# A depthwise convolution on TensorE: from full-array matmuls to sixteen 32x32 tiles

## What is computed

```python
def _L2_conv_ref(x, w77, b77, w53, b53, w35, b35, w7w, w7h, w5w, w5h):
    bias = (b77 + b53 + b35)[None, :, None, None]
    out = dwconv(x, w77, 3, 3) + dwconv(x, w53, 2, 1) + dwconv(x, w35, 1, 2) \
        + dwconv(dwconv(x, w7w, 0, 3), w7h, 3, 0) + dwconv(dwconv(x, w5w, 0, 2), w5h, 2, 0) + bias
    return out
```

## Time and profile before

| | us |
|---|---|
| median of 3 runs | 4579.74 |
| lowest, highest | 4578.52, 4580.29 |
| the profiled execution | 4581.92 |
| its span in the profile | 4580.3 |
| PE busy, share of the span | 4151.4, 91% |
| the depthwise layer in the span | about 2829 to 3219 |

### The profile page before, as it was taken

One profiled execution on the slowest core, in us unless ns is written; L12 is line 12 of the kernel. 1 busy time (PEld: TensorE's weight loads), 2 busy tenths in 40 slices (PEclk: granted clock), 3 DMA queues, 4 the chain that ended last, 5 costly groups with the idle time before them and its releaser, 6 DMA issues. The chain is left out here.

```text
span 4580.3 us, 47617 instructions
## 1 busy us (share of the span) xinstructions
PE 4151.4 (91%) x13451; PEld 2549.2 (56%) x13451; DVE 3146.5 (69%) x3239; ACT 2284.8 (50%) x3612; POOL 1357.1 (30%) x994
## 2 busy tenths in 40 slices
PE   6999999999999999569999995797499999999999
PEld 5777777777776767324344442786244444444444
DVE  4758575767676767567777663244488788888878
ACT  2858585858585858333332211211255445445544
POOL 2858585848584858121111101110000000000000
PEclk8999999999999999779999997898699999999999
DMA  4333332333332323211111011232301100110110
GB/s 129 84 100 91 94 94 92 93 95 93 93 96 85 99 83 103 77 55 42 42 42 42 28 55 58 77 113 89 145 0 41 41 15 26 41 41 0 41 41 14
DMA packets 116343, 308.02 MB, mean 67 GB/s; under 512 B 47088, under 2 KB 48752, under 8 KB 106560
## 3 DMA queue, kind: packets, MB, share of 16 engines
q1 hardware_dynamic: 110880, 294.50, 20.4%
q0 software_dynamic: 3840, 11.01, 1.1%
q10 hardware_dynamic: 1440, 0.16, 0.0%
HBM read 198.24 MB, written 106.85 MB: 67 GB/s over the span
## 5 line engine op out<-in xcount | busy, mean ns | idle before, releaser
L451 POOL TENSOR_TENSOR probs_lo<-probs,probs_hi 128x512 fp32r<-128x512 f32 x848 | 1178.5, 1404 | 651.0 <-ACT probs L497 628.6
L557 DVE TENSOR_REDUCE maxima<-m_psum 128x1 fp32r<-128x1024 f32 x528 | 644.4, 1221 | 371.9 <-PE m_psum L725 371.1
L496 ACT ACTIVATE probs_hi<-s_psum 128x512 fp32r<-128x512 f32 x1024 | 613.1, 599 | 389.0 <-PE o_psum L754 226.6
L2306 PE MATMUL psum<-mixes,conv_t 128*128 128x512 f32 x1728 | 751.1, 592 | 0.0
L497 ACT ACTIVATE probs<-s_psum 128x512 f32<-128x512 f32 x1024 | 608.7, 594 | 0.0
L2306 PEld LDWEIGHTS psum<-mixes,conv_t 128*128 128x128 f32 x1728 | 327.5, 190 | 409.8 <-issue 409.8
L738 PE MATMUL s_psum<-q_all,k_hi 128*128 128x512 f32 x1026 | 426.6, 416 | 21.5 <-ACT probs L497 21.3
L754 PE MATMUL o_psum<-probs_lo,v 128*112 128x512 f32 x1024 | 412.0, 402 | 14.6 <-DVE probs_lo L637 7.7
L739 PE MATMUL s_psum<-q_all,k_lo 128*128 128x512 f32 x1026 | 404.2, 394 | 0.0
L749 PE MATMUL o_psum<-probs_hi,v 128*112 128x512 f32 x1024 | 403.2, 394 | 0.0
L725 PE MATMUL m_psum<-k_hi,q_all 128*128 128x512 f32 x1056 | 353.6, 417 | 32.4 <-DVE maxima L557 19.2
(11 more groups left out here) (324 smaller groups left out, 6556.4 us busy)
## 6 DMA issues: line engine op xcount, KB each, us to landing
xin<-in_x SPq DMA_DIRECT2D x17, 1536.0 KB, 7.2
xin<-x SPq DMA_DIRECT2D x17, 1536.0 KB, 6.8
k_hi<-k_rows_hi SPq DMA_DIRECT2D x134, 192.0 KB, 3.4
xres<-x SPq DMA_DIRECT2D x16, 1536.0 KB, 7.1
xb<-x SPq DMA_DIRECT2D x4, 4096.0 KB, 15.9
k_rows_hi<-stage_hi SPq DMA_DIRECT2D x54, 256.0 KB, 2.1
k_rows_lo<-stage_lo SPq DMA_DIRECT2D x54, 256.0 KB, 2.3
q_rows_hi<-stage_hi SPq DMA_DIRECT2D x52, 256.0 KB, 2.5
```

Of the source, the lines that this page charges most:

```text
L451: pool.tensor_tensor(probs_lo[:, u % RING, :], probs[:, u % RING, :], as_f32(probs_hi[:, u % RING, :]), ALU.subtract).then_inc(pool_low.ne ...
L496: nc.scalar.activation(probs_hi[:, u % RING, :], s_psum[:, u % 2, :], ACT.Exp, scale=SCALE)
L557: nc.vector.tensor_reduce(maxima[:, g % 2, tile:tile + 1], source, AX.X, ALU.max, negate=True).then_inc(rows_max.next(), 1)
L2306: ins = nc.tensor.matmul(bank, conv_w[:, t, down, factor, m * P:(m + 1) * P], mixes[:, factor, t, down:down + S, :].rearrange("p a b -> p ...
```

## The change

The layer becomes one block, and its whole program is written out, without loops.

- **Convolution:** each channel and row of taps is a matmul of its own with a 32x32 band as weights: input partitions of quadrant q, output partitions of quadrant j, with j the channel number modulo 4. 16 matmuls (j, q) follow each other for a row of taps. PSUM has 2 slots of 4 banks, a bank for each q.
- **Bands** are dense, [128, 4 slots, 8, 7, 35], without zero quadrants. The transfer of a quadrant and group reads one run of 1957 elements a partition, shifted by one element from partition to partition. The rows in HBM are 35 wide, not 63.
- **Output order:** a result's partition is j * 32 + r, so the residual is loaded a second time in that order (`load_res`) and results are stored in it, 4 transfers of 32 partitions a batch. The biases are loaded in this order too, 4 transfers each.
- **Transfers** go batch by batch: 24 loads of 512 KB into a ring of 4, 24 residual loads and 24 stores through another ring of 4.
- **Buffers:** results are copied into `yt` (two slots), no longer into `xt`; all transposes to `xt` stand before all transposes back on VectorE.
- **Setup:** the moments come first on VectorE, the separable branches are 4 wider operations. GpSimd writes the padded taps itself and then loads bands, and its memset is gone.

```diff
-        bands = sb("bands", [P, 2, GROUP, TAPS, P])
-        psum = ctx.enter_context(nc.psum_tensor("psum2", [P, 4, 2, N], F32))
+        bands = sb("bands", [P, GROUPS_T, GROUP, TAPS, ROW])
+        psum = ctx.enter_context(nc.psum_tensor("psum2", [P, BANKS, 2, N], F32))
...
-            with sp.Fori(0, CT) as t:
-                sp.wait_ge(x_loaded, t * 16 + 16)
-                sp.wait_ge(stored, t * 16 + 16)
-                sp.dma_start(slot(xb, t + 1), x_tiles[bass.ds((t + 1) % CT, 1)].rearrange("a p b n -> p (a b) n")).then_inc(x_loaded, 16)
-                sp.wait_ge(out_made.sem, out_made.at(B, t))
-                sp.dma_start(out_tiles[bass.ds(t, 1)].rearrange("a p b n -> p (a b) n"), slot(xb, t)).then_inc(stored, 16)
+            def load(s):
+                if s >= RING:
+                    sp.wait_ge(normed.sem, s - RING + 1)
+                if s >= 2:
+                    sp.wait_ge(xin_loaded[s % 2], 16 * (s // 2))
+                sp.dma_start(xin[:, s % RING, :], x_tiles[s // B, s % B]).then_inc(xin_loaded[s % 2], 16)
+            def load_res(k):
+                if k >= RING:
+                    sp.wait_ge(res_moved[k % RING], res_stored(k - RING))
+                for j in range(QUADS):
+                    sp.dma_start(res[j * S:(j + 1) * S, k % RING, :], x_quads[k // B, k % B, j]).then_inc(res_moved[k % RING], 16)
+            for s in range(2 * B):
+                load(s)
+            for k in range(RING):
+                load_res(k)
+            for s in range(2 * B, STEPS):
+                load(s)
+            for k in range(STEPS):
+                sp.wait_ge(back.sem, 2 * k + 2)
+                for j in range(QUADS):
+                    sp.dma_start(out_quads[k // B, k % B, j], res[j * S:(j + 1) * S, k % RING, :]).then_inc(res_moved[k % RING], 16)
+                if k >= 1 and k + RING - 1 < STEPS:
+                    load_res(k + RING - 1)
...
+            pool.wait_ge(tap_made.sem, tap_made.at(1))
+            pool.dma_start(padded_dram[0:CT * CHANNELS].rearrange("(t p n) -> p t n", t=CT, p=P), ...
+            for n in range(CT * GROUPS_T):
+                if n >= GROUPS_T:
+                    pool.wait_ge(convolved.sem, n - GROUPS_T + 1)
+                for q in range(QUADS):
+                    pool.dma_start(target, source).then_inc(band_loaded[n % 2], 16)
...
+            def keep(t, g):
+                n = t * GROUPS_T + g
+                act.wait_ge(convolved.sem, n + 1)
+                if t >= 2:
+                    act.wait_ge(back.sem, 2 * B * (t - 1))
+                for q in range(QUADS):
+                    at = q * GROUP + 2 * g
+                    nc.scalar.copy(yt[:, t % 2, at:at + 2, :, :].rearrange("p c b h -> p (c b h)"),
+                                   psum[:, n % 2 * QUADS + q, :, :].rearrange("p c n -> p (c n)")).then_inc(kept.next(), 1)
...
+            for s in range(2 * B):
+                normalise(s)
+            for t in range(CT):
+                for g in range(GROUPS_T):
+                    if t == 1:
+                        for s in range(2 * B + 2 * g, 2 * B + 2 * g + 2):
+                            normalise(s)
+                    keep(t, g)
...
+            for s in range(STEPS):
+                turn(s)
+            dve.wait_ge(turned.sem, turned.at(STEPS))
+            for k in range(STEPS):
+                turn_back(k)
...
-                    for c in range(2):
-                        channel = 2 * n + c
-                        out = psum[:, n % 4, c, :].rearrange("p (b h) -> p b h", h=S)
-                        for k, tap in enumerate((3, 0, 1, 2, 4, 5, 6)):
-                            ins = nc.tensor.matmul(out[:, :, rows], bands[:, g % 2, channel % GROUP, tap, :],
-                                                   slot(xt, t)[:, channel, :, rows.start + down:rows.stop + down],
-                                                   start=(k == 0), stop=(k == TAPS - 1))
+                for r in range(2):
+                    for k, tap in enumerate((3, 0, 1, 2, 4, 5, 6)):
+                        for j in range(QUADS):
+                            channel = QUADS * r + j
+                            for q in range(QUADS):
+                                out = psum[j * S:(j + 1) * S, n % 2 * QUADS + q, r, :].rearrange("p (b h) -> p b h", h=S)
+                                ins = nc.tensor.matmul(out[:, :, rows], bands[q * S:(q + 1) * S, g, channel, tap, 0:S],
+                                                       xt[q * S:(q + 1) * S, t % 2, g * GROUP + channel, :, rows.start + down:rows.stop + down],
+                                                       start=(k == 0), stop=(k == TAPS - 1))
```

More of the change, by code:

```diff
@@ L1735, in _, with settled, turn @@
-            for s in (turned, back, out_made):
-                s.end_of_pass()
+            V = nc.vector
+            def settled():
+                dve.wait_ge(set_up.sem, set_up.at(set_up.count))
+            def turn(s):
+                if s >= 2 * B:
+                    dve.wait_ge(convolved.sem, (s // B - 1) * GROUPS_T)
+                dve.wait_ge(normed.sem, s + 1)
+                V.transpose(xt[:, s // B % 2, :, s % B, :].rearrange("p j h -> p h j"),
+                            xn[:, s % 2, :].rearrange("p (h j) -> p h j", j=S)).then_inc(turned.next(), 1)
@@ new lines, in _ @@
+            V.scalar_tensor_tensor(shift[:, :], moments[:, :, 0], -1.0, rstd[:, :], ALU.mult, ALU.mult).then_inc(set_up.next(), 1)
+            assert set_up.count == SHIFT_MADE
+            V.memset(padded[:, :, :, :], 0.0).then_inc(set_up.next(), 1)
+            dve.wait_ge(small_loaded, 16 * (len(taps) + QUADS * len(biases)))
+            V.tensor_tensor(bias[:, :], biases["b77"][:, :], biases["b53"][:, :], ALU.add).then_inc(set_up.next(), 1)
+            settled()
+            V.tensor_tensor(bias[:, :], bias[:, :], biases["b35"][:, :], ALU.add).then_inc(set_up.next(), 1)
@@ new lines, in _, with middle @@
+            V.tensor_copy(padded[:, :, :, LEAD:], taps["w77"][:, :, :, :]).then_inc(set_up.next(), 1)
+            settled()
+            def middle(rows, columns):
+                return padded[:, :, 3 - rows // 2:4 + rows // 2, LEAD + 3 - columns // 2:LEAD + 4 + columns // 2]
+            for n, rows, columns in (("w53", 5, 3), ("w35", 3, 5)):
+                at = middle(rows, columns)
+                V.tensor_tensor(at, at, taps[n][:, :, :, :], ALU.add).then_inc(set_up.next(), 1)
+                settled()
@@ L1757, in _ @@
-            convolved.end_of_pass()
+            nc.tensor.matmul(psum[:, BANKS - 1, 0, 0:2 * B], const["group_mean"],
+                             both[:, :, :].rearrange("p b e -> p (b e)"), start=True, stop=True).then_inc(grouped.next(), 1)
+            for n in range(CT * GROUPS_T):
+                t, g = n // GROUPS_T, n % GROUPS_T
+                if g == 0:
+                    pe.wait_ge(turned.sem, B * (t + 1))
+                pe.wait_ge(band_loaded[n % 2], 16 * QUADS * (n // 2 + 1))
+                if n >= 2:
+                    pe.wait_ge(kept.sem, QUADS * (n - 1))
+                for r in range(2):
+                    for k, tap in enumerate((3, 0, 1, 2, 4, 5, 6)):
+                        down = tap - TAPS // 2
+                        rows = slice(max(0, -down), S - max(0, down))
+                        for j in range(QUADS):
+                            channel = QUADS * r + j
[4 more added lines that the diff above has]
+                                                       start=(k == 0), stop=(k == TAPS - 1))
+                ins.then_inc(convolved.next(), 1)
```

258 lines of the change are left out of this document (97 added, 161 removed).

## The result

The changed kernel takes 4463.75 us (median of 4 runs, 4459.02 to 4468.83) beside 4580.01 us for the kernel before on the same chips: a ratio of 0.9747, 95% interval 0.973 to 0.9764. That is 116 us less, where 136 were forecast: faster as predicted, 20 us above the predicted 4444, inside the range. The profiled execution took 4468.83 us, with a span of 4467.1.

A forecast was written before the change was run, and what follows sets the result against it. Matmuls bound each pass, with chains of transfers, normalising and transposes at both ends. Gains of 93 + 26 + 8.5 + 8 = 135.5 us from 4581.92 gave 4446.4, median 2.2 lower: 4444 us; range 4350 to 4600, the forecast's own 4395 to 4530.

The forecast's parts named there:

- The convolution: Depthwise layer's matmuls on 32x32 tiles: 5376 records at 35 ns, 188 us against 281.5, a gain of 93 us.
- loads run in one stream: Convolution's weight loads come one after another at 26.6 ns; with the fixed 8.3 ns, 35 ns a record.
- rival D: Convolution at 60 to 80 ns a record, from late code or contending bands and tiles: 4580 to 4690 us; chance 0.03.
- rival C: Convolution at 13 to 25 ns a record, VectorE the bound, layer ends 229 us sooner: 4353 us; chance 0.11.
- Rival A: A matmul's two records block PE's queue, only two overlap: 563 us of convolution, 4819 us; chance 0.19.
- Rival B: Only one array direction overlaps, four tiles stream together: 52.4 ns a record, 4537 us; chance 0.17.
- some 70 us: Convolution time from the skill page's span, one matmul plus 4 ns for each further tile; near 13.1 ns a record.
- The first matmul: Layer's setup: first matmul at +32 us against +58.6, a gain of 26 us, bounds 18 and 32.
- The holes between passes: PE's holes of 4.27 and 4.18 us between the layer's passes go, a gain of 8.5 us.
- The tail: From last matmul to next layer: 33 us against 40.7, a gain of 8 us.
- no loss, but no reserve: SyncE's queue: eight issues of 0.39 us a step, 3.1 us against VectorE's 3.2.
- What would show it: Signs: record pace near 35 ns, first matmul about 32 us, no pass holes, tail under 35 us, clock under 0.9 warning.

The follow-up runs named there:

- The loop runs: Matmuls as a loop instead of written out: 448 records with fixed operands 4412.94 us; changed kernel with GpSimd-copied operands, 896 records 4437.23 us, 448 records 4408.61 us.
- the run on the diagonal: Changed kernel with all records on the four diagonal tiles instead of sixteen, channel order changed to suit: 4535.28 us.
- the loop kernel: Changed kernel with matmuls as a loop of 448 records passed twelve times, GpSimd copying channels and bands to fixed tiles, bias loads on GpSimd: 4408.61 us.
- the later profile: The changed kernel itself, run again unchanged as the measure for three other kernels: 4463.14 us, 0.9742 of the kernel before.
- without tiles: Changed kernel with full-array matmuls, 1344 records, in place of tiles, the convolution's values left out: 4539.45 us.

## Why the prediction was right, and where it was not

*The convolution: right in price by luck, wrong in mechanism.* Forecast 188 us, measured 197. I built 35 ns from a single stream of weight loads (26.6 ns) and a fixed part (8.3). The loop runs show 20.0 ns for a record with its load, so the loads were never such a stream. The other 16.6 ns are holes (68.9/5376 = 12.8) and blocks at a lower clock (3.8). The step that failed is "loads run in one stream". Code that isn't there in time was rival D, and I gave it 3% with a price of 60 to 80 ns a record; the mechanism came, at 12.8 ns of holes, on top of a faster stream. Two errors of opposite sign met at the forecast, and that is luck: with its code in place the same stream would have been near rival C. What sets 20 ns, above the 12.9 of sixteen perfect tiles, no run tells apart.

*Rival A* fell: two records of one matmul do not block the others. Two at a time would have been 563 us (even time is at 60.3 ns a record, where the prediction has 60.4). What fell is the step from strict order to only two records at any time. The order itself, which the page TensorE: Matmul & The Clock Gate of the Trainium skill has (section Packing small matmuls), no run here tests, since the rows do not say which tile a record is on. That page's span, worked out with the 209.5 ns of a record, is an estimate of (209.5 + 15 x 4)/16 = 16.8 ns a record and 91 us if each sixteen wait for the sixteen before, not the "some 70 us" of the prediction; measured are 20.0 ns in the loop. *Rival B* fell with it, and the run on the diagonal shows what it would have been: 51.7 ns and 4535 us, where 52.4 and 4537 were worked out. *Rival C* (13 to 25 ns, VectorE the bound, 4353) was true of the stream, and the loop kernels are it: at 20 ns VectorE's returns do end last. But they give 4409 and not 4353, since a step of return is 4.0 us there and not 3.2, and the returns begin only when the third tile is turned, 122 us into the layer.

*The first matmul: right.* It came at +31.7 us beside the forecast +32, a gain of 26.9. The chain is as told: shift at +12.6 (forecast +12.5), first turn at +15.8 (+16), turns done at +29.9 (+31), band loads last. One price in it was off and didn't matter: four band issues cost 4 x 0.49 us and not 4 x 0.98. That the memset was worth nothing fits, but no run isolates it.

*The holes between passes: right.* They are gone; 8.5 us.

*The tail: wrong.* Forecast 33 us, measured 42.9 (3061.1 to 3104.05), so the 8 us gained were 2 us lost; in the later profile, with 39.4, they were 1 gained. The steps that failed are "no loss, but no reserve" and that the returns "end some 20 us before" the last matmul. The issue cost was read from one row of a single 4 MB store, 0.39 us; in a row of eight they are 0.46 to 0.51, so SyncE needs 3.7 to 3.9 us a step, more than VectorE's 3.2. With the waits for the residual that follow, a step is 3.4 to 4.2 us: 31.7 us for eight, where 25.6 were forecast. The first sixteen returns, forecast to end 20 us before the last matmul, began at 2994.9 and ended at 3067.2 (4.5 us each), 3.9 us after the copies of the third tile. So no residual was loaded ahead for the last eight: in the runs on the diagonal and without tiles, where the sixteen end in time, the tail is 34 us with the same queue. The last piece, from the last addition to the next layer, is 5.2 us, near the forecast 4 and the cleanup.

*The sum.* Convolution 84.5 for 93 (281.5 less 197), first matmul 26.9 for 26, holes 8.5 for 8.5, tail -2.2 for 8: 117.7 for 135.5, and 118.1 from the layer's two edges. The layer began 3.6 us later in this execution and 1.3 us are lost behind it; its start lies between 2825.5 and 2832.5 us in all the profiles, with the same code ahead of it.

*What would show it.* The pace near 35 ns did not prove the mechanism: I had asked for its mean and not for the shape. The sign for the tail, under 35 us from the last matmul to the next layer, failed (42.9). The last sign, a clock under 0.9, did warn: 0.71 in the first 48 us.

## What to carry to other kernels

Small tiles of the array pay off, but a stream of records at 20 ns eats code faster than it comes: look for "issue" holes at even counts of instructions, and make the matmuls a loop whose body is fetched once, even if another engine must copy the operands to fixed places. Price the issue of transfers from a row with many in succession, and before moving them to another queue write down what stands ahead of them there, when that is released, and what that engine still does before it leaves the block. When a forecast's mean comes out right, look at the shape of the stream before you believe the reason.

## What the runs showed of the hardware

- Written-out fp32 matmuls on 32x32 tiles run in blocks of 128 records and stop behind each: 35 holes of up to 6.3 us, 68.9 us in all, beside 41 packets of 16 KB of code. A loop of 448 records had 3 packets in the whole convolution; a loop of 896 had 6 or 7 in every second pass and 1 or 2 in the others.
- Sixteen tiles: 20.0 ns a record of 242 columns; four diagonal tiles: 51.7 ns; the full array: 206.5 ns.
- Behind holes, the granted clock was 0.71 over 48 us, and 128 records took 4.41 us at 0.51 where they take 2.65 at 1.00.
- With the last result stores issued by GpSimd the kernel went on 11.3 us after the last addition, issued by SyncE or ScalarE some 5 us after it. The stores landed as soon; GpSimd's DRAIN at the end of the block took 8.9 us behind them.
- Eight issues a step on SyncE's queue (0.45 to 0.51 us each) gave steps of 4.0 us at 266 GB/s; with the stores on ScalarE's queue the same steps took 3.2 us at 324 GB/s.
- One 512 KB transfer whose slowest dimension is 4 ran at a DMA share of 0.26 and 105 GB/s; as four of 128 KB, with 32 rows each, 266 GB/s at 0.87.
